# Second attention of a vision tower: score and max products by strips of 32 rows, and routed rows normalized on ScalarE

## The reference

```python
def _L1_attn_ref(x, Wq, Wk, Wv, Wo, bo, q_gamma, q_beta, k_gamma, k_beta):
    q = _layernorm((x @ Wq.T).reshape(b, t, h, s), q_gamma, q_beta)      # h = 8 heads, s = 16
    k = _layernorm((x @ Wk.T).reshape(b, t, h, s), k_gamma, k_beta)
    v = (x @ Wv.T).reshape(b, t, h, s)
    scores = jnp.einsum('bqhs,bkhs->bhqk', q, k) * (1.0 / sqrt(s))
    scores = jnp.where(cols > rows, -jnp.inf, scores)
    attn = softmax(scores)
    return jnp.einsum('bhqk,bkhs->bqhs', attn, v).reshape(b, t, e) @ Wo.T + bo
# then h4 = x + that; the rows layernorm(h4) are gated (x @ Wg + bg), the two best of 8 experts
# weigh them, and silu(x @ W1 + b1) @ W2 + b2 of each chosen expert is added back
```

## Time and profile before

| | us |
|---|---|
| median of 3 runs | 1944.51 |
| lowest, highest | 1939.29, 1944.73 |
| profiled execution, its time | 1945.98 |
| profiled execution, its span | 1944.2 |

### The profile page before, as it was taken

The page is one execution under the profiler, slowest core; times in us unless marked ns, Lnnn a source line. Parts: engine busy times, 40 slices in busy tenths (PEclk is TensorE's granted clock), DMA queues, the critical chain, the costliest instruction groups (busy, mean ns, idle before and its releaser), DMA issues. The chain is left out here.

```text
span 1944.2 us, 44781 instructions
## 1 busy us (share of the span) xinstructions
PE 1670.3 (86%) x13211; PEld 1258.8 (65%) x13212; DVE 1219.6 (63%) x4791; ACT 1064.8 (55%) x2510; POOL 1138.5 (59%) x1040
## 2 busy tenths in 40 slices
PE   4999999984479763899999999999983999999995
PEld 2665666663457542476776766766762898988985
DVE  2899899983732003689999999999974222222221
ACT  2666666652445442567666667667651555555553
POOL 2455554432068873136566666666565777777776
PEclk8999999995579886899999999999995999999998
DMA  8989899932023433112112112111113676767764
GB/s 199 239 210 220 214 217 230 229 77 59 0 57 67 67 50 80 41 31 55 49 47 55 49 46 56 49 46 52 40 44 85 119 139 126 135 128 127 136 130 78
DMA packets 272309, 198.11 MB, mean 102 GB/s; under 512 B 27118, under 2 KB 252688, under 8 KB 272144
## 3 DMA queue, kind: packets, MB, share of 16 engines
q1 hardware_dynamic: 221072, 160.12, 33.0%
q0 software_dynamic: 49984, 35.38, 13.2%
q10 hardware_dynamic: 1088, 0.53, 0.1%
HBM read 143.33 MB, written 52.40 MB: 101 GB/s over the span
## 5 line engine op out<-in xcount | busy, mean ns | idle before, releaser
L2321 POOL DMA_INDIRECT out_dram<-r_yw,r_idx x212 | 328.6, 1550 | 116.2 <-issue 67.3
L2210 POOL DMA_INDIRECT rows_scratch<-routed_row,slot_u x256 | 252.0, 984 | 205.0 <-DVE slot_u L2161 141.8
L1883 ACT ACTIVATE a_probsT<-a_p_sc 98x392 f32<-98x392 f32 x384 | 170.5, 498 | 154.9 <-PE a_p_sc L1664 90.5
L2387 ACT ACTIVATE r_hT<-r_p_up,r_b1T 128x256 f32<-128x256 f32 x424 | 191.6, 474 | 114.6 <-PE r_p_up L2362 110.9
L2349 PEld LDWEIGHTS r_p_y<-w_all,r_hT 128*128 128x128 f32 x1696 | 224.0, 193 | 11.4 <-issue 0.3
L2349 PE MATMUL r_p_y<-w_all,r_hT 128*128 x1696 | 224.8, 276 | 0.0
L2362 PE MATMUL r_p_up<-r_xgT,r_w1e 128*128 128x256 f32 x848 | 221.6, 385 | 0.6 <-ACT r_xgT L2392 0.6
L448 PE MATMUL p_embed<-pix,w_pix 96*128 96x392 f32 x512 | 210.3, 518 | 3.5 <-ACT pix L567 3.5
L2403 DVE TENSOR_TENSOR r_yb<-r_p_y,b_all 128x256 f32<-128x256 f32 x106 | 45.0, 424 | 190.0 <-PE r_p_y L2349 182.1
L717 POOL TENSOR_SCALAR vare<-mv 98x4 f32<-98x4 f32 x64 | 29.9, 468 | 219.6 <-DVE mv L702 200.3
L1981 DVE TENSOR_REDUCE a_negmax<-a_p_max 98x2 bf16<-98x392 f32 x256 | 131.9, 555 | 41.1 <-PE a_p_max L1631 40.9
(11 more groups left out here) (365 smaller groups left out, 4051.3 us busy)
## 6 DMA issues: line engine op xcount, KB each, us to landing
img<-in_x_dram SPq DMA_DIRECT2D x192, 196.0 KB, 4.4
img<-in_x_dram SPq DMA_DIRECT2D x192, 189.0 KB, 4.5
r_w1e<-in_L_ffn_W_dram SPq DMA_DIRECT2D x106, 256.0 KB
r_xg<-rows_scratch SPq DMA_DIRECT2D x106, 130.0 KB, 2.4
xn_scratch<-xn SPq DMA_DIRECT2D x32, 196.0 KB
h_scratch<-h SPq DMA_DIRECT2D x32, 196.0 KB
h<-h_scratch SPq DMA_DIRECT2D x32, 196.0 KB
h3b<-h_scratch SPq DMA_DIRECT2D x32, 196.0 KB
```

The costliest lines, as they stand in the source:

```text
L1883: act.activation(probsT[:, u % 2, i, :], p_sc[i % 2][:, 0:2 * PAIR], ACT.Exp).then_inc(exped, 1)
L2210: pool.indirect_dma_start(rows_dram, bass.IndirectOffsetOnAxis(ap=slot_u[:, u % ROWS, c, t:t + 1], axis=0), row[:, u % ROWS, c, t, :], Non ...
L2321: pool.indirect_dma_start(acc_dram, bass.IndirectOffsetOnAxis(ap=idx[:, (k - 3) % 4, t:t + 1], axis=0), yw[:, (k - 3) % 4, t, :], None, co ...
L2387: act.activation(hT[:, (k - 1) % 2, f, :], p_up[f][:, 0:G], ACT.Silu, bias=b1T[:, bass.ds(e * FC + f, 1)]).then_inc(act_h, 1)
```

## The change

Three things are changed in `attend_and_route`.

1. `LIVE` is 2 and the products take strips of 32 rows, two heads each. `places` gives the pairs the strips 0 and 2, then 1 and 3. The score products are made in two parts (x = 0 and 1) in all six steps, which was so in two of them before. `score_products` and `max_products` are generators now, with one pause each, and `in_turn` takes them by turns: half of the scores, half of the max products, the other half of the scores, the other half of the max products. The two of a step always have different strips. `q_var` has two variants, so ScalarE writes two instead of four.
2. The normalized rows are `h4 * rstd + shift` with `shift = -mean * rstd`, in four ScalarE activations behind `tile(3)`. VectorE's `rows` is gone. GpSimd makes `-mean` ahead of the inverse root and `shift` behind it.
3. ScalarE's copy to the second row comes later, between the exponentials of the third and the fourth step, and `row_ready` counts both: TensorE's `turn_xn4` and the first scatters wait for 1, the scatters of the second row for 2.

```diff
-        LIVE = HEADS // 2
+        LIVE = 2
+        STRIP = 32
...
                 def places(i):
                     group, at = divmod(i, 4)
-                    half, two = divmod(ORDER[at], 2)
-                    return (0, None, 1)[group], slice(64 * half, 64 * half + 64), 2 * two, 2 * ORDER[at]
+                    strip = ORDER[at]
+                    return (0, None, 1)[group], slice(STRIP * strip, STRIP * (strip + 1)), 0, 2 * strip
...
-                    for both in zip(*spans):
+                    for k, both in enumerate(zip(*spans)):
...
+                        if 2 * k + 2 == len(spans[0]):
+                            yield
...
                     for x in range(2):
+                        if x:
+                            yield
...
-                            elif x == 0:
+                            else:
                                 o = m * PAIR
-                                pe.matmul(p_sc[p][:, 0:2 * PAIR], kT[rows, s4, o:o + TILE],
-                                          q_var[rows, s4, var:var + 2, o:o + PAIR], start=True, stop=False,
+                                pe.matmul(p_sc[p][:, x * PAIR:(x + 1) * PAIR], kT[rows, s4, o:o + TILE],
+                                          q_var[rows, s4, var + x, o:o + PAIR], start=(x == 0), stop=False,
                                           skip_group_check=True)
...
-                    if on[skew]:
-                        score_products(i, n - skew)
-                    if on[later]:
-                        max_products(j, n - later)
+                    in_turn(*([score_products(i, n - skew)] if on[skew] else []),
+                            *([max_products(j, n - later)] if on[later] else []))
...
-                    done(act, ln4, N["ln4"], u)
+                    done(act, rstd4_r, 4, u)
                     scatter_done(act, u - ROWS)
-                    act.copy(row[:, u % ROWS, 1, :, 0:D], row[:, u % ROWS, 0, :, 0:D]).then_inc(row2_ready, 1)
+                    done(act, xn4_turned, 1, u - ROWS)
+                    for t in range(TPU):
+                        last = act.activation(row[:, u % ROWS, 0, t, 0:D], h4[:, u % 2, t, :], ACT.Identity,
+                                              bias=shift4[:, u % 2, t:t + 1], scale=rstd4[:, u % 2, t:t + 1])
+                    last.then_inc(row_ready, 1)
...
-                    for t in tiles:
-                        st.mark(dve.tensor_scalar(row[:, u % ROWS, 0, t, 0:D], h4[:, u % 2, t, :],
-                                                  mv4[:, u % 2, t, 0:1], rstd4[:, u % 2, t:t + 1],
-                                                  ALU.subtract, ALU.mult))
```

More of the change, by code:

```diff
@@ L1952, in emit @@
                 exps(2, 4, 4)
+                if on[6]:
+                    u = n - 6
+                    done(act, row_ready, 2, u, 1)
+                    act.copy(row[:, u % ROWS, 1, :, 0:D], row[:, u % ROWS, 0, :, 0:D]).then_inc(row_ready, 1)
                 exps(4, 6, 4)
@@ L2094, in emit @@
                                     ).then_inc(aux_ready, 1)
-                rows((0, 1, 2, 3))
                 maxes(0, 2, 3)
@@ L2178, in dve_emit @@
             dve.tensor_scalar(gains[:, 0:2], gains[:, 0:2], float(HD) ** -0.5, None, ALU.mult).then_inc(wcp, 1)
-            dve.tensor_tensor(var_of[:], head_of[:, 0:LIVE], head_of[:, LIVE:HEADS], ALU.add).then_inc(wcp, 1)
+            dve.tensor_reduce(var_of[:], head_of[:].rearrange("p (s v) -> p v s", v=LIVE), X, ALU.add
+                              ).then_inc(wcp, 1)
             dve.wait_ge(wcp, 2)
@@ L2224, in emit @@
                     done(pool, ln4, N["ln4"], u, 9, apart=True)
-                    inverse_root(rstd4[:, u % 2, :], vare4[:, u % 2, :], mv4[:, u % 2, :, 1], 1.0, rstd4_r, 2 * u)
+                    done(pool, row_ready, 2, u - 2, 1)
+                    pool.tensor_scalar(minus4[:], mv4[:, u % 2, :, 0], -1.0, None, ALU.mult).then_inc(rstd4_r, 1)
+                    inverse_root(rstd4[:, u % 2, :], vare4[:, u % 2, :], mv4[:, u % 2, :, 1], 1.0, rstd4_r, 4 * u + 1)
+                    wait(pool, rstd4_r, 4 * u + 3)
+                    pool.tensor_tensor(shift4[:, u % 2, :], minus4[:], rstd4[:, u % 2, :], ALU.mult
+                                       ).then_inc(rstd4_r, 1)
                 scatter((5, 6, 7), 8)
```

24 lines of the change are left out of this document (8 added, 16 removed).

## The result

The changed kernel took 1939.76 us in the median of 20 runs, the kernel before, beside it on the same chip, 1945.05. The ratio is 0.9977, with a 95% interval of 0.9968 to 0.9985. The gain is about 5 us where 33 were forecast, and it lies outside the range: **the prediction was wrong in size and right in sign on this chip**. On a second chip the same two kernels came out with the other sign (1.0261), and on two more chips kernels with most of the change were slower than before too, as the experiments show.

A forecast was written before the change was run, and what follows sets the result against it. VectorE and TensorE waiting on each other bound the kernel; the period falls from 20.83 to 13.43 + 6.30 = 19.73 us. About 28 periods give 31 us, the first ones 2, filling and draining cancel: 33 us, 1911 us; range 1895 to 1936.

The forecast's parts named there:

- the ring: Second attention, steady unit: VectorE and TensorE each wait for the other once per unit; two arcs, 14.46 + 6.37 = 20.83 us.
- VectorE's arc: VectorE's stretch from its idle wait through maxima reductions until TensorE is released; 14.46 us falls to 13.43 without the normalizations.
- The wait in step 5: Fifth of a unit's six scores_and_max calls: TensorE waits for maxima, half the scores queued behind; gain 0.07 us, not 0.27.
- GpSimd's two operations: Negated mean and shift on GpSimd: 0.19 us each, done before ScalarE asks, so no cost.
- The strips' term: Each step's products on four strips: max products' 0.27 us hidden under the scores' 0.74; bounds 0.74 and 1.01.
- step 3: Third scores_and_max call of a unit, where TensorE's max products wait for VectorE's maxima; TensorE had 0.34 us in hand.
- The rows' term: Four row activations on ScalarE: 0.29 us apart, 1.26 until the last ends; TensorE waits about 0.45 us.
- it just keeps up: TensorE's margin at step 3 after the change: 0.34 + 1.18 - 1.03 - 0.45 = 0.04 us.
- TensorE's arc: From VectorE's release at step 3 to the mask products that release VectorE again; 6.37 us now, 6.30 forecast.
- the change moves the wait only: Rival: ScalarE's rows come 1 us later than thought, TensorE is late at step 3, gain lost: 1944 us; chance 0.05.
- The ends: Pipeline ends: first periods gain 0.7 us each, 2 in all; filling gains 1 us, draining loses 1.
- The slower rival: Each change of strips costs an array refill of 0.08 us, a step's products take 1.25: 1978 us; chance 0.10.

The follow-up runs named there:

- the chip of the third question: Chip of the last follow-up kernels, on which cutting score products was tested apart from strips; the kernel before took 1962.43 us there.
- the uncut kernel: Changed kernel with each score product whole, 392 columns instead of two of 196, still in strips of 32 rows: 1964.94 us, ratio 1.0016 to the kernel before.
- wide ends: Changed kernel with halves of 64 rows for units 0, 1, 2, 30 and 31, strips for the other 27: 1987.37 us, ratio 1.0115 to the kernel before.
- the last two kernels: Changed kernel with rows turned behind the weighted sums and 64-row halves at both ends: 1973.57 us, 1.0064; the same with uncut score products: 1937.82 us, 0.9871.
- the chip of the second question: Chip where the unchanged pair was rerun: the kernel before took 1966.76 us, the changed kernel 2013.61 us, ratio 1.0261.

## Why the prediction was wrong, point by point

**The views and the ring held.** The kernel is bound where the prediction put it. VectorE's arc became 13.33 us on the first chip (13.43 forecast). The wait in step 5 came as described: the maxima of step 4 end at 1033.55 + 1.04 = 1034.59, the max products start at 1034.65 with half of the scores queued behind them, and `aux` starts at 1035.16, 0.57 us after the release where the prediction's terms make 0.53. VectorE idles 0.88 us ahead of step 5, in the 0.6 to 0.9 named. GpSimd's two operations cost nothing.

**The strips' term was too good.** A step's products take 0.84 us, not 0.74: 0.17 of the 0.27 are hidden. The bounds 0.74 and 1.01 held it. Over the three steps ahead of step 3 that is 0.30 us of what TensorE was to have in hand. The Trainium skill, "TensorE: Matmul & The Clock Gate", Part 3, has 3.07 as the speedup of four row tiles, which gave 0.96 us as an estimate; the measurement lies between that and full hiding.

**The rows' term was too good as well, and "it just keeps up" is the step that failed in steady work.** The nearest row had a scale per partition alone, and from it I took 0.29 us from one row activation to the next, 1.26 for all four and 0.45 us of waiting. The activations, which have a bias too, follow each other by 0.385 us, the prediction's upper bound, and all four take 1.68; TensorE loses 0.93 - 0.17 = 0.76 us. With the measured sizes the prediction's own sum for step 3 reads 0.34 + 3 x 0.17 + 0.37 - 1.03 - 0.76 = -0.57 where it had 0.04: TensorE does not "just keep up", it is late, and step 3 runs all its products after it arrives. Of these 0.61 us the rows are 0.31 and the strips 0.30. TensorE's arc is 0.51 us longer than forecast, about this amount. The period gains 0.69 instead of 1.10, and 0.41 x 28 = 11.5 us of the forecast are gone. Turning the rows behind the weighted sums takes the wait away. Where instructions come late it brought the period from 21.58 to 21.1. On the chip of the third question the uncut kernel has 20.56 with the early rows and 19.88 with late ones and wide ends, with a TensorE arc of 6.35 us; not all of these 0.68 are the rows', since the late instructions of step 5 went too. On the first chip this was not tried. The prediction named this as a rival, "the change moves the wait only", with the full 1.03 lost and 5% of the chance; it was a partial case of it.

**The ends had no term for the clock.** The first period was forecast to gain 0.7 us and lost 5.5; draining was to lose 1 and lost 10.3. Together that is some 15.5 us. I read "a granted clock of 1.00" off the steady unit and carried it to all units. The row to read was there: in the earlier trace rows the first stretch has TensorE busy for 14.88 of 18.00 us, at 0.99, and in the 13.50 us right before it the clock was 0.50, the lower level. The rows do not say that strips would bring it down, only that the level is not safe there. That the strips do it is shown for the first period by the kernel with cut and turns but no strips against the one with strips and no cut (19.15 us and 0.94 against 23.49), and that it costs what it seems to cost by the wide ends (first period 23.4 to 19.1 us, draining 75.2 to 68.7). For the draining the share of strips and cut is open.

Added up: 33 forecast, less 11.5 for the rows, less 15.5 for the ends, leaves 6; the spans differ by 3.0, the medians by 5.3. So the small gain is the sum of a gain in steady work and a loss at the ends that nearly cancel; that its sign was right is in part luck.

**The cut had no term, and the chip none either.** On the three slower chips every kernel with cut score products has weighted sums that end about 0.9 us late in each period. It costs 26 us without strips (1988.36 against 1962.43 of before, turns included) and 36 between the last two kernels, which differ by it alone, and it turns the sign. On the first chip the changed kernel has the cut and doesn't lose the 0.9 us. Nothing in the trace of before shows it: that kernel's weighted sums take 1.14 us on either kind of chip. What was visible is that the change adds 512 matmuls and as many weight loads to an engine that is already busy for 20.42 of 20.83 us, and I priced them at nothing since they stream the same columns.

**The slower rival** (a refill at each change of strips, 1978 us) named a wrong mechanism. A step takes 0.84 us, not 1.25. Its 1.7% more is nearer to what the changed kernel shows on the chip of the second question (2.6% more) than my forecast is, by accident.

## What to carry to other kernels

Cutting matmuls into smaller ones for the sake of their order costs instructions, and here that cost more than the order brought (36 us on a slower chip); first see whether the array overlaps them anyway. Price an operation that changes its engine by a row of the same shape on the new engine, and where only a distant row exists, put the consumer as late as its engine allows, so that the error costs nothing. Read the granted clock in each stretch of a pipeline, not in the steady one alone, and where a kernel is to run on many chips, measure small changes on more than one.

## What the hardware showed that I had not expected

- By the trace's starts, matmuls on different strips start out of the program's order: max products queued behind eight score matmuls start 0.03 us after the first of these (997.46 against 997.43).
- With strips of 32 rows the granted clock falls where halves of 64 rows keep it: first period 0.65 to 0.67 against 0.92 to 0.99, though TensorE is busier in time (21.3 us of 23.5 against 14.9 of 18.0). Adding matmuls on the idle strips brought 0.75. What the chip reacts to remains open.
- In draining, strips with cut products run at 0.50 to 0.55 and strips with uncut ones at 0.99 over the first 20 us, in one trace each. No experiment here explains that.
- TensorE's instructions can come late with no releaser in the trace. With cut score products (13723 matmuls and more) three chips lose 0.9 us in the weighted sums of each period and one doesn't. With uncut ones (13211) three kernels lose nothing there, and a fourth, the strips uncut, 0.15 us, and 0.3 more in step 5. So the cut brings most of it, as the last two kernels show, which differ by it alone. Whether it is the number of instructions or their shortness, why the chips differ, and why it strikes in these places, is open. The kernel that beats the one before was timed only on a chip of the slower kind.
